# The last three down products of the quantised feed-forward layer, made one step later on TensorE

## The reference, cut to what matters

```python
x = x + tanh(g_xattn[0]) * L0_xattn(layernorm(x), ctx)     # 32 query heads, 8 key/value heads of 128
x = x + tanh(g_ffn[0])   * L0_ffn(layernorm(x))            # 1376 hidden units
x = x + tanh(g_xattn[1]) * L1_xattn(layernorm(x), ctx)
x = x + tanh(g_ffn[1])   * L1_ffn(layernorm(x))

# L0_ffn: every operand is rounded to a block float (blocks of 32) before its product
gate, up = fp6(x) @ fp4(w_gate).T, fp6(x) @ fp4(w_up).T
return fp6(silu(gate) * up) @ fp4(w_down).T                # the down products
```

## Time and profile before

| | |
|---|---|
| time, median of 3 runs | 1316.86 us (1316.17 to 1316.87) |
| the profiled execution | 1317.38 us, span 1315.6 us |
| PE busy | 1301.6 us, 99% of the span |
| DVE busy | 1002.2 us, 76% |
| ACT busy | 866.9 us, 66% |
| POOL busy | 621.4 us, 47% |
| granted TensorE clock | 1.0 |

### The profile page before, as it was taken

The page is one execution under the profiler, slowest core; times in us unless marked ns, Lnnn a source line. Parts: engine busy times, 40 slices in busy tenths (PEclk is TensorE's granted clock), DMA queues, the critical chain, the costliest instruction groups (busy, mean ns, idle before and its releaser), DMA issues.

```text
span 1315.6 us, 25535 instructions
## 1 busy us (share of the span) xinstructions
PE 1301.6 (99%) x7493; PEld 1102.0 (84%) x7493; DVE 1002.2 (76%) x2106; ACT 866.9 (66%) x3356; POOL 621.4 (47%) x683
## 2 busy tenths in 40 slices
PE   8999999999999999999999999999999999999999
PEld 7888888888888888877777788888888888888887
DVE  6878788787878788688888858777667677676756
ACT  5767667676767776645566456777767777676651
POOL 2546566565646566446677533532323323232232
PEclk9999999999999999999999999999999999999999
DMA  7011110111121011020301013623222122321001
GB/s 298 1 56 57 63 56 20 66 50 68 50 68 50 24 68 47 13 64 20 103 20 48 20 48 89 161 65 73 64 66 70 36 71 61 80 56 33 17 9 57
DMA packets 87338, 78.29 MB, mean 60 GB/s; under 512 B 70881, under 2 KB 75873, under 8 KB 83169
## 3 DMA queue, kind: packets, MB, share of 16 engines
q1 hardware_dynamic: 70272, 71.91, 18.6%
q10 hardware_dynamic: 16672, 4.46, 1.6%
q0 software_dynamic: 320, 1.05, 0.2%
HBM read 57.48 MB, written 3.15 MB: 46 GB/s over the span
## 4 chain that ended last, share of the span: by engine, by line
PE 84%; DVE 5%; issue 5%; DMA 2%; POOL 2%; ACT 1%; ACTq 0%; POOLq 0%; DVEq 0%; SPq 0%
PE bank L1298 60%; PE bank L1364 7%; PE bank L1290 7%; PE bank L1395 6%; PE bank L1326 2%; DMA p_turned<-p_planes 1%; PE bank L1381 1%; PE bank L1479 1%; POOL rstd L580 1%; DMA f_iqT<-f_iq 1%; DVE probs L1138 1%; ACT squares L769 0%; DMA ctx_raw<-in_ctxT 0%; DVE f_q L975 0%; DVE amax L968 0%
## 5 line engine op out<-in xcount | busy, mean ns | idle before, releaser
L551 POOL TENSOR_TENSOR w_lo<-w_raw,w_hi (+1 forms) x150 | 192.7, 1301 | 163.9 <-ACT w_hi L730 163.9
L769 ACT ACTIVATE squares<-bank 128x128 bf16<-128x128 f32 x512 | 134.4, 278 | 184.6 <-PE bank L1298 184.5
L711 ACT ACTIVATE probs<-probs,negmax 128x128 f32<-128x128 f32 x512 | 198.2, 391 | 7.0 <-DVE negmax L1010 4.5
L576 POOL TENSOR_TENSOR meansq<-sumsq,scalars 128x5 f32<-128x5 f32 x128 | 27.5, 215 | 352.5 <-ACT squares L769 352.5
L580 POOL TENSOR_TENSOR rstd<-meansq,scalars 128x5 f32<-128x5 f32 x128 | 152.9, 1194 | 10.7 <-POOL meansq L576 1.1
L1298 PE MATMUL bank<-w_hi,oT_hi 128*128 (+1 forms) x512 | 150.9, 416 | 0.0
L1298 PE MATMUL bank<-w_hi,xT_hi 128*128 (+1 forms) x512 | 140.1, 395 | 0.0
L1298 PE MATMUL bank<-w_lo,xT_hi 128*128 (+1 forms) x512 | 138.1, 390 | 0.3
L1364 PEld LDWEIGHTS bank<-kT,qT 128*128 128x128 f32 x1024 | 131.7, 191 | 7.7
L1298 PE MATMUL bank<-w_hi,oT_lo 128*128 (+1 forms) x512 | 138.0, 391 | 0.0
L1298 PE MATMUL bank<-w_lo,oT_hi 128*128 (+1 forms) x512 | 137.6, 390 | 0.0
(11 more groups left out here) (129 smaller groups left out, 3000.2 us busy)
## 6 DMA issues: line engine op xcount, KB each, us to landing
w_raw<-in_wq SPq DMA_DIRECT2D x16, 1024.0 KB, 4.8
w_raw<-in_wo SPq DMA_DIRECT2D x16, 1024.0 KB, 9.6
w_raw<-in_wkv SPq DMA_DIRECT2D x16, 512.0 KB, 5.6
fw_raw<-in_ffn_w SPq DMA_DIRECT2D x36, 192.0 KB, 2.3
x_sb<-in_x SPq DMA_DIRECT2D x7, 256.0 KB, 10.4
ctx_raw<-in_ctxT SPq DMA_DIRECT2D x7, 256.0 KB, 9.8
fw_raw<-in_ffn_w SPq DMA_DIRECT2D x7, 256.0 KB, 2.6
out<-x_sb SPq DMA_DIRECT2D x7, 256.0 KB, 2.0
```

Source lines behind the costliest of these rows:

```text
L551: last = nc.gpsimd.tensor_tensor(lo, raw, hi.bitcast(FP32), ALU.subtract)
L576: nc.gpsimd.tensor_tensor(meansq[:, :], sumsq[:, :], eps_sb[:, :], ALU.add).then_inc(ms_done, 1)
L711: last = nc.scalar.activation(probs[:, h * P:(h + 1) * P], probs[:, h * P:(h + 1) * P], ACT.Exp, bias=negmax[:, h:h + 1], accum_out=rowsum ...
L769: last = nc.scalar.activation(squares[:, h // 2, (b + 1) % 4, h % 2, :], q_bank(n, kind)[:, h * P:(h + 1) * P], ACT.Square, scale=SCALE, a ...
```

## The change

The first 8 of the 11 down products stay at the end of the `down` step. The last three, those of chunk 2, are issued in the following step, between that step's k and v products and its q products; `d_ps` is incremented behind them. Nothing is added or removed, and no other engine's code changes.

```diff
+            def down_products(i, chunks):
+                for k, (r, rows) in enumerate(ITILES):
+                    c = sum(r >= first for first in CHUNK_STARTS) - 1
+                    if c not in chunks:
+                        continue
+                    if r in CHUNK_STARTS:
+                        pe.wait_ge(iT_sb[c], 16 * (i + 1))
+                    col = (DOWN_BLOCK + KT * k) * P
+                    last = nc.tensor.matmul(psC[:, :], f_iqT[0:rows, k, :], wT[0:rows, col:col + D],
+                                            start=(k == 0), stop=(k == NT - 1))
+                return last
...
                     three_products(psKV[:, 0:2 * P], lambda a, k: (ctx_hi, ctx_lo)[a][:, batch, k * P:(k + 1) * P],
                                    lambda a, k: weights(0, WKV0 + k * 2 * P, 2 * P)[a]).then_inc(kv_ps, 1)
+                if t.acc is not None:
+                    down_products(t.acc, (2,)).then_inc(d_ps, 1)
                 if has(n, 0) and kind != FIRST:
...
                 if t.down is not None:
                     wait(pe, d_acc, t.down)
-                    for k, (r, rows) in enumerate(ITILES):
-                        if r in CHUNK_STARTS:
-                            pe.wait_ge(iT_sb[CHUNK_STARTS.index(r)], 16 * (t.down + 1))
-                        col = (DOWN_BLOCK + KT * k) * P
-                        last = nc.tensor.matmul(psC[:, :], f_iqT[0:rows, k, :], wT[0:rows, col:col + D],
-                                                start=(k == 0), stop=(k == NT - 1))
-                    last.then_inc(d_ps, 1)
+                    down_products(t.down, (0, 1))
```

## The result

The changed kernel takes 1318.73 us (median of 20 runs, 1317.74 to 1321.09); the kernel before, run beside it, 1316.62 (20 runs, 1315.9 to 1320.43). The ratio is 1.0017, with a 95% interval of 1.0011 to 1.0023: slower by 2.1 us, which is real but within what the forecast counted as no change. The prediction was 1319.1.

The account below looks back on a forecast made before the run. PE bounds the kernel, without slack against the DVE-POOL-DVE chain in five steps. Delay +3.2, less 0.4 and 0.2 absorbed, gives +2.6; less 0.35 gives +2.25, so 1319.1 us, counted as no change; range 1316.8 to 1322.6.

Parts of the forecast that it names:

- (a) What it frees: PE's transpose waits for chunk 2: 1.29 us in step 18, given back in step 19, and 0.35 in step 22.
- (b) What it delays: `d_ps` later, DVE's line 1081 waits 0.8 us; through POOL, PE loses 0.8 in steps 13, 15, 17, 21: +3.2.
- (c) What the chain takes up: DVE's hold under POOL's normalisation shrinks: about 0.4 us absorbed in step 15, 0.2 in 13, 17, 21; sum +2.6.
- the 0.06: Amount in us taken off the delay in each of steps 13, 17 and 21, where POOL's start moves with the chain.
- (d) Switching: PE changes between bf16 and fp32 twice more per tile: taken as 0, upper bound 0.18 us per tile.
- (e) Step 22: Step 23 has cover, so the transpose wait freed in step 22 stays gained: -0.35 us.
- The signs: Expected in the new profile: DVE waiting in seven tiles, longer weight-load waits, named windows; plus readings that would prove it wrong.
- Freed and kept: Rival: DVE's wait does not reach PE in the five steps, only the freed time counts; 1316.5 to 1315.2, chance 0.14.
- The switches cost: Rival: each extra bf16/fp32 switch on PE takes 0.18 us; 1320.3, chance 0.10.
- Caught one after the other: Rival: POOL's normalisation holds DVE's lines 969, 971, 974 each; 3.8 us over five steps, 1322.9, chance 0.14.
- Blocked to POOL's end: Rival: DVE's three small instructions wait for POOL's whole normalisation in steps 13 to 21; 9 us, 1325.8, chance 0.05.

Follow-up runs that it names:

- pad_before: Kernel before, PE's order kept, with one more DVE read of 128x512 ahead of its wait for `d_ps`; 1318.91 us, ratio 1.0017.
- rstd_first_after: Changed kernel with POOL's two small instructions on the new moments moved behind the attention's `rstd`; 1315.29 us, ratio 0.9988 to before.
- rstd_first_before: Kernel before with POOL's two small instructions on the new moments moved behind the attention's `rstd`; 1315.52 us, ratio 0.9989.
- pieces17_after: Changed kernel with POOL's two late weight pieces of step 18 split in step 17, behind its other two; 1321.62 us, ratio 1.0039 to before.
- all_late: Changed kernel with all eleven down products, not just three, behind the next step's k and v products; 1323.11 us, ratio 1.0050 to before.

## Why the prediction was right

**(a) What it frees.** Right. The wait for the transpose is gone, and it gave nothing in steps 18 and 19 together (+0.03), since step 19 takes it back. This 0 was forecast. By the starts of the k and v products, step 18 is 1.93 shorter and step 19 1.96 longer, of which 0.65 are the three products themselves. DVE came to line 1081 of step 19 at 688.65, after the products' end at 687.97, and did not wait, as forecast. PE's wait for line 975 in step 19 is the longest of the five (timelines of DVE and PE):

```profile
698.40 0.47 DVE L969 TENSOR_SCALAR amax<-amax 128x16 f32<-128x16 f32 x1
...
699.94 1.04 PE L1326 MATMUL bank<-wT,f_xqT 128*128 128x512 bf16 x4 [0.91 <-DVE f_q L975]
```

The prediction took DVE's late arrival in step 19 from its row and did not say where it comes from. It comes from POOL's two pieces in step 18: without them and without the chain at POOL the stretch takes 26.94 with the new order. With the order of before that pair of edits was not run.

**(b) What it delays.** Right, link by link, as the rows of step 13 above show: DVE starts line 1081 at 605.46, the time forecast, 0.81 after that of before, after 0.68 of idle time (it had itself come free 0.13 later). Two small errors cancel in that time: the products end at 605.42, not 605.37, and DVE starts 0.04 behind them, where the forecast took 0.09 from POOL. Against the even start it is 0.76. POOL's `ln_var`, `rstd` and DVE's `qn` are 0.83 later each by the clock. Steps 13, 17 and 21 lost 0.71, 0.70 and 0.73, for a forecast of 0.74. Both ends were shown by experiments: the delay alone (pad_before) brings the loss, and the chain cut at POOL (rstd_first_after) takes it away with the delay still there.

**(c) What the chain takes up.** Right, in size and in the how. In step 15 the forecast had 0.4 absorbed, and 0.43 of 0.8 came through. The prediction had POOL's start set by PE, and so it is: 24.76 after the even start before, 24.78 now. By "the block" it meant the time for which POOL holds DVE up, to 0.80 after POOL's start, and not the three small instructions, whose end went from 25.57 after the even start to 25.99. The rows (timelines of POOL and DVE, step 15) show both:

```profile
642.25 2.08 POOL L570 TENSOR_SCALAR qn<-x_sb,ln_mv,ln_rstd 128x512 f32<-128x512 f32 x1 [2.20 <-PE bank L1290]
...
642.87 0.18 DVE L969 TENSOR_SCALAR amax<-amax 128x16 f32<-128x16 f32 x1
643.08 0.17 DVE L971 TENSOR_SCALAR inv_pow<-amax 128x16 uint32<-128x16 uint32 x1
643.29 0.17 DVE L974 TENSOR_SCALAR blk_pow<-amax 128x16 uint32<-128x16 uint32 x1
```

Line 969 came 0.62 after POOL's start and ended 0.80 after it, just where the hold ends, so it lost nothing, and the two behind it took what they take with POOL idle. What is given back is the 0.38 that line 974 lost before. In step 13 line 969 came 0.32 after POOL's start and was held to 615.72, for a forecast of 615.7. So there the loss of before is taken over by another line and nearly nothing given back, as the 0.06 said.

**(d) Switching.** Right: with the waits gone, two steps take 26.77 with the new order (rstd_first_after) and 26.76 with the old (rstd_first_before).

**(e) Step 22.** Right in the number, -0.32 for -0.35, but no run shows that the move earns it. pad_before, in which nothing moved, gains the same 0.34 in this window and shows no wait for the transpose in step 22. In rstd_first_before, with the old order, the window is 26.92, and 26.76 with the new one, so there the move is worth 0.16. The wait in step 22 is short and differs from one kernel to the next; the prediction read it from one trace.

**The signs.** DVE waits in seven tiles and not in step 19, the weight loads wait 1.18, 1.18 and 1.18 in steps 13, 17 and 21, 0.88 in 15 and 1.40 in 19, and the window from step 13 to 15 is 27.61: all as named. Lines 969 to 974 take 0.89 together in step 13, below the 1.1 that would have shown the forecast wrong. Two signs did not fit. The window from 17 to 19 was to stay near 28.2 and is 27.62; that from 19 to 21 is 28.22 instead of 26.90. By the prediction's own sum it had to be so, since the 1.29 freed in step 18 leave the first of the two and come back in the second: the sum was right and the sign was not worked out from it. And busy PE above 26.75 was to show the forecast wrong. It is 26.80 to 26.82 in the windows of steps 12 to 17. But it is 26.90 there in the kernel before, which counts the small waits as busy, so this sign could not tell anything.

**The rivals.** "Freed and kept" fell with PE's 3.4 of waits. Even with the chain cut the change keeps nothing: -1.06 in the windows against -1.08 with the old order. "The switches cost" fell by (d). "Caught one after the other" did not happen where it was feared, in the `acc` steps of the changed kernel: there only line 969 was held. It happened already in step 18, under the two pieces, before and after alike, in pieces17_after, and in step 19 of rstd_first_after across a piece and the normalisation (timelines of POOL, DVE and PE):

```profile
695.20 2.54 POOL L551 TENSOR_TENSOR w_lo<-w_raw,w_hi 128x512 fp32r<-128x512 f32 x2
...
697.13 0.63 DVE L969 TENSOR_SCALAR amax<-amax 128x16 f32<-128x16 f32 x1
...
697.72 2.08 POOL L570 TENSOR_SCALAR qn<-x_sb,ln_mv,ln_rstd 128x512 f32<-128x512 f32 x1
697.80 0.71 DVE L971 TENSOR_SCALAR inv_pow<-amax 128x16 uint32<-128x16 uint32 x1
...
699.38 0.82 PE L1326 MATMUL bank<-wT,f_xqT 128*128 128x512 bf16 x3 [0.67 <-DVE f_q L975]
```

"Blocked to POOL's end" fell for the normalisation, and holds for the pieces (below). Its price was out of line with the other rivals': it put the 9 us on the time before, 1316.8, and left out the -0.35.

## What to carry to other kernels

A wait that the profile names as PE's only DMA wait may hide a chain that ends at the same moment; before moving work, follow what the moved work releases, engine by engine, to the next place where the bound engine waits, and ask as well what it covered where it stood. A short instruction that waits at the head of an in-order queue (here POOL's `ln_var`, 0.19 us) passes its whole delay to everything behind it: letting the urgent result go first was worth 1.1 us by itself and took away all that the move had cost. A longer wait of TensorE can cost more than its own length, so look at the granted clock behind it. Move such work only as far as the reader is late anyway: behind four products it was free, behind twelve it cost 2, behind twenty-four 21.

## What was not expected of the hardware

- How long DVE's short instructions are held depends on what POOL runs. Under POOL's normalise (2.08 us, line 570) line 969 or 971 of DVE ended 0.78 or 0.79 after its start each time (615.72 after 614.93, 698.51 after 697.72), and one that came 0.62 after it took its usual 0.18, which brought it to 0.80 as well. Under `w_lo` (1.25 us each, line 551) they were held to its end: line 971 in pieces17_after took 1.19 and ended 0.03 after the fourth piece, and in step 18 of the changed kernel it took 1.22 and ended 0.04 after the second. The two differ in operation and operands, and no run varies these one at a time, so why they differ is open. The SBUF — State Buffer page of the Trainium skill, "Who interferes with whom", says that when VectorE in a 2-port mode and GpSimd meet, the one that issues first gets the shared ports for its whole instruction and the other is blocked. The trace agrees for `w_lo` and not for the normalise.
- Pieces in a row each catch one short instruction: as soon as one is let go the next is held, so that three instructions of together 0.6 us can take 2.4 (pieces17_after, 670.10 to 672.47).
- TensorE's granted clock was at 0.50 for 3.4 us behind a wait of 2.17 us in pieces17_after. In the same stretch of the other kernels, whose longest wait is 1.61 (all_late), it stayed at 1.00. One case was seen.
- Two more changes between bf16 and fp32 products per tile were free in sum (26.77 against 26.76 us for two steps).
